# Second expert layer: chunks prepared rank by rank, table work later on VectorE, and 32 identity products ahead of the second half's counts

## Chip, cores and metric

One core of one Trainium2 chip. The metric is the time of one execution in device microseconds; for each kernel the median of the timed runs counts.

## What is computed

The input is x of 8 x 128 tokens with 256 features, and a context of the same shape. Four layers follow one another, each added to x: a long convolution over the features (by Toeplitz products), a mixture of 8 experts (2 per token), a cross attention with a latent width of 64, and a second mixture of 32 experts. The change is in that last layer:

```python
w, idx = _gate(xf, gate_w)            # sigmoid scores, 4 of 8 groups, then 6 of 32 experts
c = jnp.zeros((T, E), xf.dtype).at[jnp.arange(T)[:, None], idx].add(w)
g = jnp.einsum('td,eid->tei', xf, w11)
u = jnp.einsum('td,eid->tei', xf, w33)
act = jax.nn.silu(g) * u
y = jnp.einsum('tei,te,edi->td', act, c, w22)
shared = jax.nn.silu(xf @ sw1.T) * (xf @ sw3.T) @ sw2.T
return (y + shared).reshape(x.shape)
```

There T is 1024 tokens, E is 32, and an expert's hidden width is 128.

## The kernel before, in words

The kernel is written engine by engine, with every order and every semaphore by hand: one block each for SyncE (`sp`, which issues the loads), GpSimd (`pool`), ScalarE (`act`), VectorE (`dve`) and TensorE (`pe`).

**Routing.** Tokens are routed in two halves of four blocks. For each half TensorE makes the logits (`logits`, L1684), ScalarE the sigmoid, VectorE the choice of six experts a token (`choose`, ending in the mask at L1316), and TensorE counts how many rows stand ahead of each one (`count_rows`, L1712 and L1717). VectorE makes slots from the counts (`later_slots` for the second half, first instruction L1124). A token's six chosen experts, in the order of the expert's number, are its ranks 0 to 5. For each rank of a half, `stage_values` (L1161 to L1168) makes the slots and gate values, and GpSimd sends the four blocks' rows to DRAM by four indirect transfers (`send_rows`, L688). The sends of the second half are numbered 6 to 11, one per rank; before rank 3, 4 or 5 is staged, the rank three before it must have been sent, since they share a buffer.

**Chunks.** The rows of an expert lie in chunks of 224 (two tiles of 112). The first 32 chunks are the first of each expert, and their order is fixed. Chunk k holds only tokens of rank k or lower, so chunks 0 to 4 need the ranks up to their own number, and all chunks from 5 on need all six (`wait_sent`). Each chunk is one step s = 4i + r of a loop that all engines run (`run_steps`):

- SyncE loads the chunk's rows (`rowbuf`) and its weights (`up_raw`, `down_raw`; for experts 11 to 22 these were loaded early into buffers of their own).
- TensorE turns the rows (`turn_rows`, L1784); ScalarE copies the turned rows and the up weights to a short format (L843, L848, `high_parts`), and VectorE keeps the rests (L1416, L1421, `low_parts`). This is the preparation of a chunk.
- TensorE makes gate and up products (`up`, twelve products at L1664 to L1666); ScalarE applies silu (L870); VectorE copies the rows' targets (`place`, L1434) and multiplies (`hid`, L1443); TensorE makes the down product (`down`, L1817); ScalarE scales the results (`take_y`, L857), and GpSimd sends them back to the tokens' places in DRAM (L726), two transfers a chunk.

In the steady loop, TensorE's step s is: up of s, turn of s + 2, down of s - 1. The copy to `place` waits until the results of the chunk four before have been sent, since they read that buffer.

**What stands around the change.** Before the loop VectorE stages the second half's ranks (numbers 6 to 11), multiplies the shared expert's hidden values (`shared_hid`, L1373), adds the shared expert's output to x (`add_shared`, L1381), and works out which experts need a second chunk (`table_sums`, `table_turns` from L1202, `table_codes` from L1224 to L1239; the tables are read after 24 chunks). Only then come the preparations of chunks 0 and 1 (`low_parts`). TensorE makes the shared expert's products (`shared_up`, `shared_down` at L1749), waits until all of them have been added to x, because the second turned chunk shares a bank with them, and turns chunks 0 and 1 one after the other. In step r of the first four, it does up r, down r - 1, turn r + 2. The function `keep_busy` (L1742) multiplies the identity by itself into a bank that nobody reads; it is called twice before, with six products each.

Of the kernel before, what the change touches and what calls it, by code (L numbers as in the profile page):

```python
# [49 lines left out]
def build(nc, x_d, ctx_d, ctxr_d, filt_d, skip_d, wr_d, up0_d, down0_d, theta_d, theta_b_d, phi_d, phi_b_d, g_d, g_b_d,  # L50
# [11 lines left out]
    with ExitStack() as stack:  # L62
# [241 lines left out]

        def run_steps(eng, n, step):

            for i in range(FIXED[n]):
                for r in range(4):
                    step(i, r, i == 0, False)
            turns, more = load_turns(eng, n)  # L310
            with eng.Fori(FIXED[n], more + (MINT[n] - 1)) as i:
                for r in range(4):
                    step(i, r, False, False)
            for r in range(4):
                step(more + (MINT[n] - 1), r, False, True)
            return turns

        def prepared(n):

            def ahead_of(r, prepare):
                if n == 0 and r < 2:
                    for t in range(2 * r):
                        prepare(t)
                else:
                    prepare(r)

            return ahead_of

        def is_zero(count):
# [95 lines left out]
        def _(sp):  # L427
# [41 lines left out]
            for n in range(2):  # L469
# [70 lines left out]
                def step(i, r, first, last):  # L540
# [5 lines left out]
                    down_src = None if own else of_unit(down_d, here, r % upe)  # L546
                    if not (last and r >= 2):
                        c, first_unit, _, cslot, _ = chunk_of(n, i, r, 2)
                        slot, _ = step_slot(i, r, 2)
                        up_src, rows_src = None if own_later else of_unit(up_d, later, r % upe), rows_of(region)  # L550
                        if not first:

                            sp.wait_ge(f.w_split, s - 1)
                        elif r >= 2:
                            sp.wait_ge(f.w_split, r - 1)
                            if upe == 1:
                                sp.wait_ge(f.x_split, r - 1)
# [8 lines left out]
                    if not first and not own:  # L566
                        sp.wait_ge(f.down_done, s - 3)
                        load(down_raw[r][:], down_src, f.down_in[r])
# [183 lines left out]
        def _(act):  # L752
# [56 lines left out]
            for n in range(2):  # L809
# [52 lines left out]
                high_parts(0, 0, 0)  # L862
                high_parts(0, 1, 0)

                def step(i, r, first, last):
                    s = 4 * i + r
                    if n == 0 and first and r == 2:
                        take_y(i, r, -1)
                    act.wait_ge(f.up_done, s + 1)
                    nc.scalar.activation(silu_g[r % 2][:, 0:CHUNK[n]], gate_up(n, r % 2)[0][:, 0:CHUNK[n]], ACT.Silu)\  # L870
                        .then_inc(f.silu_made, 1)
                    if first:
                        if r and not (n == 0 and r == 2):
                            take_y(i, r, -1)
# [121 lines left out]
        def _(dve):  # L996
# [386 lines left out]
            for n in range(2):  # L1383
                f, upe = ffns[n], UPE[n]
                ahead_of = prepared(n)
                if n == 0:
                    for c in range(4):
                        split_rows(0, c)
                    route_first()
                else:  # L1390
                    stage_values(6)
                    shared_hid(1)
                    stage_values(7)
                    stage_values(8)
                    shared_hid(2)
                    table_sums(1, 2)
                    stage_values(9)
                    shared_hid(3)
                    add_shared(0)
                    table_turns(1, 2)  # L1400
                    stage_values(10)
                    add_shared(1)
                    stage_values(11)
                    table_codes(1)

# [17 lines left out]

                low_parts(0, 0, 0)
                low_parts(0, 1, 0)

                def step(i, r, first, last):
# [16 lines left out]
                    ins.then_inc(f.hid_made, 1)  # L1444
                    if first:
# [4 lines left out]
                turns = run_steps(dve, n, step)  # L1450
                last_k = TOPK[n] - 1
# [173 lines left out]
        def _(pe):  # L1625
# [128 lines left out]
            for n in range(2):  # L1754
# [14 lines left out]
                if n == 1:  # L1769
# [4 lines left out]
                    shared_down(3)  # L1774
                    pe.wait_ge(x_added, X_ATT1 + 4)

# [46 lines left out]
                turn_rows(0, 0, 0)  # L1823
                if upe == 1:
                    turn_rows(0, 1, 0)

                def turn_later(i, r):
                    c, first_unit, _, _, _ = chunk_of(n, i, r, 2)
# [3 lines left out]
                    turn_rows(i, r, 2)  # L1832

                def step(i, r, first, last):
                    if first:
                        if n == 0 and r == 2:
                            down(i, r, -1)
# [145 lines left out]
                shared_down(0)  # L1983
                logits(1)
                count_rows(1, slice(4, B), RANKS[1][1], 3)

# [54 lines left out]
```

## Time and profile before

| What | us |
|---|---|
| three timed runs | 410.45, 412.38, 405.9 |
| their median | 410.45 |
| the profiled execution's own time | 408.52 |
| its span, from first to last instruction | 406.7 |

The span is read from the first to the last instruction of one execution; the time of that execution is 1.8 us longer. Over the span the mean granted clock of TensorE was 0.849 of 2.4 GHz, where the levels are 2.4 and 1.2 GHz. TensorE is busy 71% of the span, VectorE 63%, GpSimd 52%, ScalarE 41%. The convolution layer ends near 68 us, the first expert layer near 179 us, the attention and the routing of the second layer near 300 us, and the rest is the loop over 32 chunks and the sum at the end.

### The profile page before, as it was taken

Reading aid. Unit: us, or ns where it says so; the run is one execution under the profiler, and the core shown is the slowest. Engines: PE = TensorE matmul, PEld = TensorE weight load, DVE = VectorE, ACT = ScalarE, POOL = GpSimd, SP = SyncE. Lnnn points to the kernel's source line nnn. Section 1 sums busy time; section 2 is a strip of 40 time slices with the busy share of each in tenths; the row PEclk is TensorE's granted clock in tenths of the full one; section 3 lists DMA queues with packets and bytes.
Section 4 is the critical chain, followed back from the end, with each engine's and each line's share of the span. In section 5 each row is a group of like instructions: output and inputs, shape, how many; then the busy total and the mean of one; then the engine's idle time right before and its main releaser. Section 6 shows DMA issues by size and latency. Waiting matters only on the chain.

```text
span 406.7 us, 5245 instructions
## 1 busy us (share of the span) xinstructions
PE 287.6 (71%) x1471; PEld 216.1 (53%) x1471; DVE 257.0 (63%) x758; ACT 167.7 (41%) x368; POOL 211.5 (52%) x238
## 2 busy tenths in 40 slices
PE   0899975610699999339899396583579899999600
PEld 0444433310679888026466174462569799998400
DVE  4499998570253533175886878798645566656366
ACT  1500003530255554525636534220266688887400
POOL 2577751037433555410511077767775677778830
PEclk9999997655599999958967778789598999999955
DMA  8556699723376651489989222325469855798598
GB/s 236 163 139 180 178 271 270 222 84 116 124 218 196 187 175 50 147 282 319 305 256 365 78 79 92 106 89 178 146 182 289 250 168 156 240 283 274 176 374 283
DMA packets 66062, 80.56 MB, mean 198 GB/s; under 512 B 7643, under 2 KB 55061, under 8 KB 66035
## 3 DMA queue, kind: packets, MB, share of 16 engines
q1 hardware_dynamic: 56547, 62.45, 52.2%
q0 software_dynamic: 7296, 16.93, 12.2%
q10 hardware_dynamic: 2192, 0.86, 0.8%
q8 instruction: 12, 0.20, 0.2%
q14 instruction: 15, 0.12, 0.1%
HBM read 43.70 MB, written 38.01 MB: 201 GB/s over the span
## 4 chain that ended last, share of the span: by engine, by line
PE 52%; DVE 15%; DMA 11%; POOL 10%; issue 7%; ACT 4%; POOLq 1%; SPq 0%; ACTq 0%; DVEq 0%
PE banks L1817 9%; POOL rows_s L688 7%; PE banks L1664 6%; PE banks L1665 5%; PE banks L1666 5%; DMA y_s<-y_sb,place 4%; PE banks L1784 4%; PE banks L1645 4%; PE banks L1646 3%; PE banks L1647 3%; PE banks L1674 2%; POOL y_s L726 2%; DMA rowbuf<-rows_s 2%; PE banks L1910 2%; DMA pre_own<-y_s 2%
## 5 line engine op out<-in xcount | busy, mean ns | idle before, releaser
L726 POOL DMA_INDIRECT y_s<-y_sb,place x88 | 90.8, 1032 | 47.1 <-ACT y_sb L857 24.1
L688 POOL DMA_INDIRECT rows_s<-staged,slot_i x64 | 64.2, 1003 | 57.2 <-DVE staged L1168 38.9
L1664 PE MATMUL banks<-xT_hi,w_hi 128*128 128x224 f32 (+1 forms) x192 | 63.8, 332 | 8.2 <-DVE w_lo L1421 8.0
L1665 PE MATMUL banks<-xT_lo,w_hi 128*128 128x224 f32 (+1 forms) x192 | 56.5, 294 | 0.0
L1666 PE MATMUL banks<-xT_hi,w_lo 128*128 128x224 f32 (+1 forms) x192 | 56.4, 294 | 0.0
L1664 PEld LDWEIGHTS banks<-xT_hi,w_hi 128*128 128x128 f32 x192 | 38.5, 201 | 13.9 <-DVE w_lo L1421 10.9
L1817 PE MATMUL banks<-down_raw,hid 128*104 128x256 f32 (+1 forms) x176 | 44.0, 381 | 1.6 <-DVE hid L1443 1.4
L1784 PE MATMUL banks<-ident,rowbuf 112*128 112x112 f32 (+1 forms) x176 | 25.3, 275 | 27.2 <-DMA rowbuf<-rows_s 22.7
L765 ACT ACTIVATE h_sb<-x_sb,shift,rstd 128x256 f32<-128x256 f32 x22 | 11.7, 590 | 68.8 <-DVE shift L1027 68.8
L857 ACT ACTIVATE y_sb<-banks,meta 112x256 f32<-112x256 f32 (+1 forms) x88 | 36.3, 471 | 8.0 <-PE banks L1817 7.5
L1665 PEld LDWEIGHTS banks<-xT_lo,w_hi 128*128 128x128 f32 x192 | 38.5, 201 | 0.7
L640 POOL TENSOR_TENSOR kv<-ctxr_sb 128x512 f32<-128x512 f32 x32 | 32.6, 1041 | 11.4 <-PE banks L1647 11.4
L1666 PEld LDWEIGHTS banks<-xT_hi,w_lo 128*128 128x128 f32 x192 | 38.4, 200 | 0.0
L843 ACT ACTIVATE xT_hi<-banks 128x448 fp32r<-128x448 f32 (+1 forms) x40 | 22.9, 573 | 36.1 <-PE banks L1784 34.7
L870 ACT ACTIVATE silu_g<-banks 128x224 f32<-128x224 f32 (+1 forms) x48 | 18.3, 381 | 44.6 <-PE banks L1666 44.6
L1784 PEld LDWEIGHTS banks<-ident,rowbuf 112*128 112x128 f32 (+1 forms) x176 | 19.9, 151 | 28.9 <-DMA rowbuf<-rows_s 20.1
L1817 PEld LDWEIGHTS banks<-down_raw,hid 128*104 128x104 f32 (+1 forms) x176 | 28.1, 173 | 7.2 <-DVE hid L1443 1.7
L1413 DVE COPY meta<-rowbuf 112x4 f32<-112x4 f32 (+1 forms) x40 | 7.3, 183 | 34.2 <-ACT xT_hi L843 21.8
L1434 DVE COPY place<-meta 112x2 int32<-112x2 int32 (+1 forms) x40 | 7.6, 191 | 33.7 <-DMA y_s<-y_sb,place 17.1
L619 POOL TENSOR_TENSOR rstd<-veps,minus_half 128x4 f32<-128x4 f32 x8 | 8.6, 1070 | 38.6 <-DVE veps L1021 38.6
L1416 DVE TENSOR_TENSOR xT_lo<-banks,xT_hi 128x448 fp32r<-128x448 f32 (+1 forms) x40 | 26.1, 654 | 0.0
L1421 DVE TENSOR_TENSOR w_lo<-up_raw,w_hi 128x512 fp32r<-128x512 f32 x36 | 24.4, 683 | 0.0
(241 smaller groups left out, 595.5 us busy)
## 6 DMA issues: line engine op xcount, KB each, us to landing
rows_s<-empty SPq DMA_DIRECT2D x5, 2730.0 KB
up_raw<-in_up SPq DMA_DIRECT2D x38, 256.0 KB, 4.7
rowbuf<-rows_s SPq DMA_DIRECT2D x32, 227.5 KB, 3.4
down_raw<-in_down SPq DMA_DIRECT2D x38, 128.0 KB, 4.6
rows_s<-empty SPq DMA_DIRECT2D x7, 633.8 KB
rowbuf<-rows_s SPq DMA_DIRECT2D x8, 316.9 KB
toep<-filt_s SPq DMA_DIRECT2D x16, 128.0 KB, 3.3
h_sb<-y_s SPq DMA_DIRECT2D x4, 512.0 KB, 5.3
```

Of the source, the lines that this page charges most:

```text
L640: last = nc.gpsimd.tensor_tensor(kv[slot][:, blk].rearrange("p (b i j) -> p b i j", i=HD, j=HD), k, v, ALU.mult)
L688: nc.gpsimd.indirect_dma_start(out=rows_s, out_offset=bass.IndirectOffsetOnAxis(ap=slot_i[:, k, b:b + 1], axis=0), in_=staged[:, b, k % BU ...
L726: nc.gpsimd.indirect_dma_start(out=y_s[n], out_offset=bass.IndirectOffsetOnAxis(ap=place[slot][0:TILE[n], t:t + 1], axis=0), in_=y_sb[slot ...
L843: nc.scalar.activation(xT_hi[par][:, 0:KB * CHUNK[n]].rearrange("p (k c) -> p k c", k=KB), turned(n, par), ACT.Copy)\
L857: last = nc.scalar.activation(y_sb[slot][0:TILE[n], t], y_home(n, slot % 2, t), ACT.Copy, scale=meta[slot][0:TILE[n], t, 0:1])
L1416: nc.vector.tensor_tensor(xT_lo[par][:, cols].rearrange("p (k c) -> p k c", k=KB), turned(n, par), xT_hi[par][:, cols].bitcast(f32).rearra ...
L1421: nc.vector.tensor_tensor(w_lo[slot % 2][:], up_home(n, c, slot), w_hi[slot % 2][:].bitcast(f32), ALU.subtract).then_inc(f.w_split, 1)
L1664: nc.tensor.matmul(out, wh, xh, start=start, stop=False)
L1665: nc.tensor.matmul(out, wh, xl, start=False, stop=False)
L1666: return nc.tensor.matmul(out, wl, xh, start=False, stop=stop)
L1784: last = nc.tensor.transpose(turned(n, slot % 2)[:, k, t * TILE[n]:(t + 1) * TILE[n]], rowbuf[slot][0:TILE[n], t, k * P:(k + 1) * P], iden ...
L1817: last = nc.tensor.matmul(y_home(n, cslot % 2, t), hid[slot % 2][:, t * TILE[n]:(t + 1) * TILE[n]], down_home(n, c, slot), start=first_uni ...
```

## The change

It has four parts.

1. TensorE gets 32 products of the identity (`keep_busy`) between the second half's logits and its counts. They write to the bank of the counts, which is overwritten by them.
2. The first six chunks are prepared rank by rank, on TensorE, ScalarE and VectorE (`by_rank`, `prepares`). Only chunk 0 is prepared ahead of the loop. Step 0 prepares chunk 1, step 1 chunk 2, step 2 chunk 3, step 3 chunk 4, step 4 chunks 5 and 6 with chunk 4's down product between them, and step 5 chunk 7. TensorE's wait for the shared expert's sum now stands behind chunk 0's up products.
3. On VectorE chunk 0's split stands ahead of stage number 10, and all of step 0 ahead of stage number 11. The two table pieces are moved into the loop, behind steps 8 and 10.
4. SyncE asks for chunk 5's up weights and chunk 4's down weights before it waits for rank 5, no longer after it.

```diff
+        def by_rank(n, i, r):
+            return n == 1 and isinstance(i, int) and 4 * i + r < TOPK1
+        def prepares(i, r):
+            return ((1,), (1,), (1,), (1,), (1, 2), (2,))[4 * i + r]
...
 # SyncE
-                    if not (last and r >= 2):
+                    if n == 1 and first and r == 3:
+                        sp.wait_ge(f.w_split, 2)
+                        load(up_raw[1][:], of_unit(up_d, TOPK1 - 1, 0), f.up_in[1])
+                        sp.wait_ge(f.down_done, 1)
+                        load(down_raw[0][:], of_unit(down_d, TOPK1 - 2, 0), f.down_in[0])
+                        sp.wait_ge(f.x_split, 2)
+                        wait_sent(TOPK1 - 1)
+                        load(rowbuf[1][0:TILE[n], 0:TILES[n]], rows_of(TOPK1 - 1), f.rows_in[1])
+                    elif not (last and r >= 2):
...
 # ScalarE
+                    if by_rank(n, i, r):
+                        if 0 < s < TOPK1 - 1:
+                            take_y(i, r, -1)
+                        high_parts(i, r, prepares(i, r)[0])
+                        if s == TOPK1 - 2:
+                            take_y(i, r, 0)
+                            high_parts(i, r, 2)
+                        return
...
 # VectorE
-                    add_shared(0)
-                    table_turns(1, 2)
-                    stage_values(10)
-                    add_shared(1)
-                    stage_values(11)
-                    table_codes(1)
...
+                    if by_rank(n, i, r):
+                        for ahead in prepares(i, r):
+                            low_parts(i, r, ahead)
...
+                    if n == 1 and isinstance(i, int) and s == 8:
+                        table_turns(1, 2)
+                    if n == 1 and isinstance(i, int) and s == 10:
+                        table_codes(1)
...
+                    add_shared(0)
+                    low_parts(0, 0, 0)
+                    stage_values(10)
+                    add_shared(1)
+                    step(0, 0, True, False)
+                    stage_values(11)
...
 # TensorE
-                    pe.wait_ge(x_added, X_ATT1 + 4)
...
-                if upe == 1:
-                    turn_rows(0, 1, 0)
...
+                    if by_rank(n, i, r):
+                        s = 4 * i + r
+                        up(i, r, first)
+                        if 0 < s < TOPK1 - 1:
+                            down(i, r, -1)
+                        if s == 0:
+                            pe.wait_ge(x_added, X_ATT1 + 4)
+                        turn_later(i, r, prepares(i, r)[0])
+                        if s == TOPK1 - 2:
+                            down(i, r, 0)
+                            turn_later(i, r, 2)
+                        return
...
                 logits(1)
+                keep_busy(RANKS[1][1], 32)
                 count_rows(1, slice(4, B), RANKS[1][1], 3)
```

TensorE before, from the shared expert's last down products (`down_raw,hid` 128x256) over the turns (`ident,rowbuf`) to chunk 0's up products:

```order
L1749 MATMUL banks<-down_raw,hid 128x256 x8
L1784 MATMUL banks<-ident,rowbuf 128x112 x8
L1664 MATMUL banks<-xT_hi,w_hi 128x224
L1665 MATMUL banks<-xT_lo,w_hi 128x224
L1666 MATMUL banks<-xT_hi,w_lo 128x224
```

The same place now:

```order
L1786 MATMUL banks<-down_raw,hid 128x256 x8
L1820 MATMUL banks<-ident,rowbuf 128x112 x4
L1701 MATMUL banks<-xT_hi,w_hi 128x224
L1702 MATMUL banks<-xT_lo,w_hi 128x224
L1703 MATMUL banks<-xT_hi,w_lo 128x224
```

Eight turns, of chunks 0 and 1, have become four, of chunk 0; chunk 1's stand behind chunk 0's twelve up products.

VectorE before, from the sum of the shared expert's first half (`x_sb,banks`) over the first table instructions (`expert_f` and others):

```order
L1381 TENSOR_TENSOR x_sb<-x_sb,banks 128x512 x2
L1202 TENSOR_TENSOR expert_f<-sums_T 1x38
L1203 TENSOR_SCALAR expert_f<-expert_f 1x38
L1204 TENSOR_SCALAR is_last<-expert_f 1x38
L1205 TENSOR_TENSOR expert_f<-expert_f,is_last 1x38
L1206 TENSOR_TENSOR total_f<-cend 1x1
```

The same place now, with chunk 0's split and the start of stage number 10:

```order
L1408 TENSOR_TENSOR x_sb<-x_sb,banks 128x512 x2
L1425 COPY meta<-rowbuf 112x4
L1428 TENSOR_TENSOR xT_lo<-banks,xT_hi 128x448
L1433 TENSOR_TENSOR w_lo<-up_raw,w_hi 128x512
L1393 COPY staged<-ids 128x4
L1188 SCALAR_TENSOR_TENSOR pick<-nth,slot_f 128x128
```

The table instructions have gone from here, and the split of chunk 0 (`xT_lo`, `w_lo`) has come from behind stage 11. Where the table instructions stand now, behind chunk 10's split in step 8 and ahead of chunk 9's `place` and `hid`:

```order
L1433 TENSOR_TENSOR w_lo<-up_raw,w_hi 128x512
L1229 TENSOR_TENSOR expert_f<-sums_T 1x38
L1230 TENSOR_SCALAR expert_f<-expert_f 1x38
L1231 TENSOR_SCALAR is_last<-expert_f 1x38
L1232 TENSOR_TENSOR expert_f<-expert_f,is_last 1x38
L1233 TENSOR_TENSOR total_f<-cend 1x1
L1237 SCALAR_TENSOR_TENSOR extra_f<-chunk_no 1x38
L1239 SCALAR_TENSOR_TENSOR expert_f<-expert_f,extra_f 1x38
L1242 TENSOR_SCALAR extra_f<-chunk_no 1x15
L1243 TENSOR_SCALAR extra_f<-extra_f,total_f 1x15
L1244 TENSOR_REDUCE more_f<-extra_f 1x1
L1246 TENSOR_SCALAR last_f<-more_f 1x1
```

Eleven instructions of the table stand within a step of the loop; nine more (`table_codes`) stand two steps later in the same way.

## Rows read from the trace of the kernel before

**Rows 1.** GpSimd's timeline: start us, us, engine, line, operation [idle before, releaser].
```profile
268.72 1.15 POOL L688 DMA_INDIRECT rows_s<-staged,slot_i  x1 [1.93 <-DVE staged L1168]
...
298.77 1.37 POOL L688 DMA_INDIRECT rows_s<-staged,slot_i  x1 [0.30 <-issue]
300.44 0.97 POOL L726 DMA_INDIRECT y_s<-y_sb,place  x1 [0.30 <-ACT y_sb L857]
...
326.17 0.94 POOL L726 DMA_INDIRECT y_s<-y_sb,place  x1 [0.72 <-ACT y_sb L857]
...
329.16 0.94 POOL L726 DMA_INDIRECT y_s<-y_sb,place  x1 [0.30 <-issue]
```

**Rows 2.** The chain of waits, in order of time: start us, us, what.
```profile
301.71 2.87 DMA rowbuf<-rows_s
...
312.44 7.32 DMA y_s<-y_sb,place
...
389.62 5.67 DMA y_s<-y_sb,place
```

**Rows 3.** TensorE's timeline, chunks 0, 4, 5, 6 and 9.
```profile
290.81 0.55 PE L1664 MATMUL banks<-xT_hi,w_hi 128*128 128x224 f32 x1 [4.72 <-DVE w_lo L1421]
...
304.72 0.98 PE L1784 MATMUL banks<-ident,rowbuf 112*128 112x112 f32 x4 [2.40 <-DMA rowbuf<-rows_s]
305.38 0.54 PE L1664 MATMUL banks<-xT_hi,w_hi 128*128 128x224 f32 x1
...
308.03 0.55 PE L1784 MATMUL banks<-ident,rowbuf 112*128 112x112 f32 x4
...
309.09 0.45 PE L1664 MATMUL banks<-xT_hi,w_hi 128*128 128x224 f32 x1
...
311.68 0.46 PE L1664 MATMUL banks<-xT_hi,w_hi 128*128 128x224 f32 x1
...
321.56 0.37 PE L1664 MATMUL banks<-xT_hi,w_hi 128*128 128x224 f32 x1
```

**Rows 4.** VectorE's timeline: first and last of both table pieces; chunks 6 and 7.
```profile
278.92 0.18 DVE L1202 TENSOR_TENSOR expert_f<-sums_T 1x38 f32<-1x38 f32 x1
...
281.03 0.14 DVE L1219 TENSOR_SCALAR last_f<-more_f 1x1 f32<-1x1 f32 x1
...
287.33 0.38 DVE L1224 TENSOR_SCALAR is_last<-chunk_no,last_f 1x38 f32<-1x38 f32 x1
...
289.41 0.14 DVE L1239 CAST more_i<-more_f 1x1 int32<-1x1 f32 x1
...
313.79 0.17 DVE L1434 COPY place<-meta 112x2 int32<-112x2 int32 x1 [0.72 <-ACT silu_g L870]
...
319.85 0.35 DVE L1434 COPY place<-meta 112x2 int32<-112x2 int32 x1 [4.20 <-DMA y_s<-y_sb,place]
```

**Rows 5.** Busy time by stretch; behind GpSimd's: granted clock, DMA share, GB/s.
```profile
255.00:260.00 5.00, 1.06 (x10) 0.95 (x9) 4.02 (x29) 2.68 (x4) 3.78 (x5) 1.00 0.28 101
...
300.00:305.00 5.00, 2.60 (x20) 2.13 (x19) 1.66 (x5) 2.39 (x6) 3.78 (x5) 0.96 0.58 176
305.00:310.00 5.00, 5.00 (x31) 4.85 (x30) 2.56 (x8) 2.81 (x7) 2.21 (x3) 0.70 1.03 290
```

**Rows 6.** TensorE's timeline: six identity products, what follows them, and the counts.
```profile
239.70 1.51 PE L1742 MATMUL banks<-ident 128*128 128x128 f32 x12
241.14 1.98 PE L1929 MATMUL banks<-tx,outw_sb 64*128 64x512 f32 x4
...
260.96 0.47 PE L1712 MATMUL banks<-mask_r,before_r 128*128 128x128 f32 x1 [4.89 <-DVE mask_r L1316]
```

**Rows 7.** VectorE's timeline: its first use of the counts.
```profile
263.17 0.19 DVE L1124 TENSOR_SCALAR cend<-banks 128x32 f32<-128x32 f32 x1 [0.62 <-PE banks L1717]
```

**Rows 8.** The page's costliest groups: line, engine, operation, count | busy us, mean ns | idle before.
```profile
L843 ACT ACTIVATE xT_hi<-banks 128x448 fp32r<-128x448 f32 (+1 forms) x40 | 22.9, 573 | 36.1 <-PE banks L1784 34.7
...
L1421 DVE TENSOR_TENSOR w_lo<-up_raw,w_hi 128x512 fp32r<-128x512 f32 x36 | 24.4, 683 | 0.0
```

More of the change, by code:

```diff
@@ L303, in chunk_of, with run_steps @@
             return 2 * i + t // 2, t % 2 == 0, t % 2 == 1, (t // 2) % 2, i + t // 4
-        def run_steps(eng, n, step):
+        def run_steps(eng, n, step, begun=0):
             for i in range(FIXED[n]):
-                for r in range(4):
+                for r in range(0 if i else begun, 4):
                     step(i, r, i == 0, False)
@@ L322, in ahead_of @@
             def ahead_of(r, prepare):
[L323 to L327, printed above, removed]
-            return ahead_of
+                for t in range(2 * r) if r < 2 else (r,):
+                    prepare(t)
+            return ahead_of
+        def by_rank(n, i, r):
+            return n == 1 and isinstance(i, int) and 4 * i + r < TOPK1
+        def prepares(i, r):
+            return ((1,), (1,), (1,), (1,), (1, 2), (2,))[4 * i + r]
         def is_zero(count):
@@ L565, in step @@
                             load(up_raw[slot][:], up_src, f.up_in[slot])
-                    if not first and not own:
+                    if not first and not own and not (n == 1 and isinstance(i, int) and s == TOPK1 - 2):
                         sp.wait_ge(f.down_done, s - 3)
@@ L862, in _ @@
                 high_parts(0, 0, 0)
-                high_parts(0, 1, 0)
+                if n == 0:
+                    high_parts(0, 1, 0)
                 def step(i, r, first, last):
@@ L871, in step @@
                         .then_inc(f.silu_made, 1)
+                    if by_rank(n, i, r):
[6 more added lines that the diff above has]
+                        return
                     if first:
-                        if r and not (n == 0 and r == 2):
+                        if r and r != 2:
                             take_y(i, r, -1)
@@ L1389, in _ @@
                     route_first()
[L1390 to L1398, printed above, removed]
-                    add_shared(0)
-                    table_turns(1, 2)
-                    stage_values(10)
-                    add_shared(1)
-                    stage_values(11)
-                    table_codes(1)
                 def low_parts(i, r, ahead):
@@ L1422, in low_parts @@
                                             ALU.subtract).then_inc(f.w_split, 1)
-                low_parts(0, 0, 0)
-                low_parts(0, 1, 0)
                 def step(i, r, first, last):
@@ L1444, in step @@
                     ins.then_inc(f.hid_made, 1)
-                    if first:
+                    if by_rank(n, i, r):
+                        for ahead in prepares(i, r):
+                            low_parts(i, r, ahead)
+                    elif first:
                         ahead_of(r, lambda t: low_parts(i, t, 2))
@@ L1448, in step @@
                         low_parts(i, r, 2)
-                turns = run_steps(dve, n, step)
+                    if n == 1 and isinstance(i, int) and s == 8:
+                        table_turns(1, 2)
+                    if n == 1 and isinstance(i, int) and s == 10:
+                        table_codes(1)
+                if n == 0:
+                    low_parts(0, 0, 0)
+                    low_parts(0, 1, 0)
+                else:
+                    stage_values(6)
+                    shared_hid(1)
+                    stage_values(7)
+                    stage_values(8)
+                    shared_hid(2)
+                    table_sums(1, 2)
+                    stage_values(9)
+                    shared_hid(3)
+                    add_shared(0)
+                    low_parts(0, 0, 0)
+                    stage_values(10)
+                    add_shared(1)
+                    step(0, 0, True, False)
+                    stage_values(11)
+                turns = run_steps(dve, n, step, n)
                 last_k = TOPK[n] - 1
@@ L1823, in _, with turn_later @@
                 turn_rows(0, 0, 0)
-                if upe == 1:
-                    turn_rows(0, 1, 0)
-                def turn_later(i, r):
-                    c, first_unit, _, _, _ = chunk_of(n, i, r, 2)
+                def turn_later(i, r, ahead=2):
+                    c, first_unit, _, _, _ = chunk_of(n, i, r, ahead)
                     back = (1, 2)[n]
@@ L1831, in turn_later @@
                         pe.wait_ge(f.x_split, c - back + 1)
-                    turn_rows(i, r, 2)
+                    turn_rows(i, r, ahead)
                 def step(i, r, first, last):
+                    if by_rank(n, i, r):
[10 more added lines that the diff above has]
+                        return
                     if first:
-                        if n == 0 and r == 2:
+                        if r == 2:
                             down(i, r, -1)
```

## The prediction

> **What bounds the kernel now.** I read the chain of waits first, then the timelines of GpSimd, TensorE and VectorE between 255 and 330 us, and last the windows. No engine is full over the span, so the question is which one each stretch waits for.
>
> From 268.72 to 300 us it is GpSimd. It sends the second half's rows to their slots, six ranks of four transfers, back to back: the first at 268.72 after a wait of 1.93 us for VectorE, the last at 298.77, the first result row at 300.44 [rows 1]. From first to last that is 23 steps in 30.05 us, 1.31 us each (1.27 where nothing disturbs), so a rank comes every 5.1 to 5.2 us. Chunk k of the expert loop needs ranks 0 to k. Chunk 5, the last that waits for a rank, starts its load at 301.71 and takes 2.87 us [rows 2]; TensorE waits 2.40 us for it and turns it at 304.72 [rows 3].
>
> Meanwhile TensorE loses time that costs nothing yet: it multiplies chunk 0 only at 290.81, after 4.72 us of waiting for VectorE's splits, which stand behind its table work [rows 3]. But when chunk 5's rows are there, chunk 4's up products (305.38 to 308.03, at the low clock) still stand ahead of chunk 5's, which start at 309.09 [rows 3]. That work could lie in the wait. From there a chunk takes 2.59 us (309.09 to 311.68) [rows 3].
>
> Behind it comes a second loss. Chunk 7's hidden product needs the place buffer that chunk 3's results leave; they are sent at 312.44, take 7.32 us [rows 2], and VectorE stands 4.20 us until 319.85 [rows 4]. TensorE should have begun chunk 9 at 309.09 + 4 x 2.59 = 319.45 and begins at 321.56 [rows 3]: 2.1 us lost. The transfers are slow because the DMA engines are full in this stretch (share 1.03 of their time) [rows 5].
>
> From chunk 9 on GpSimd works without waiting: it still waits 0.72 us for chunk 8's results (326.17), none from 329.16 on [rows 1], and the last result transfer leaves at 389.62 [rows 2]. So TensorE's delays of some tenths behind chunk 9 are hidden by GpSimd, while a head start at chunk 8 is passed on to the end.
>
> **The change, part by part.** *The 32 products.* They stand on TensorE between the second half's logits and its counts. The counts start at 260.96, after 4.89 us idle, so the logits end near 256.0 [rows 6]. A product of the identity is two records: six of them took 239.70 to 241.14 at full clock, 0.24 us each [rows 6]. 32 of them: 7.7 us, from 256.0 to 263.7. That is 2.7 us past the time at which the mask is there. The counts then run at full clock. Now VectorE gets them 2.21 us after their start (260.96 to 263.17) [rows 6, 7]; at twice the clock between 1.1 and 2.2 us, I take 1.2, near the half, because nine short products are nearly all of it. VectorE starts on them at 264.9 instead of 263.17: 1.7 us late (bounds 1.6 and 2.7). It had waited only 0.62 us for the counts [rows 7], so a quicker count alone could have given at most that. All that follows on VectorE up to the first send is one chain, so GpSimd's 24 sends shift by 1.7 us: chunk 5's rows are loaded at 306.3 instead of 304.6. The shared expert's products behind the counts run at full clock, but nothing waits for them in this stretch.
>
> The Trainium skill prices these products differently. "TensorE: Matmul & The Clock Gate", section "Back-to-back issue gap", gives some 81 ns for a sustained product with 128 columns; by it 32 take an estimated 2.6 us, end within the idle 4.89 us and cost nothing. Its figure belongs to two-byte operands; these are four-byte ones, and the row above decides.
>
> *Chunks rank by rank.* Up 0 no longer waits for the tables; each of the first chunks is turned when its rows land. One chunk's cycle, up, down before it, turn, copies and splits, from rows: up 1.53 us (2.59 less the 1.06 from 308.03 to 309.09, which are turn and down [rows 3]), down 0.7 of these; then ScalarE copies the results (some 0.9) and the turned rows (0.57), and VectorE splits the rows and the weights (0.68 for the weights [rows 8], the rows about as long), 2.8 us with the turn hidden beside them. That is 5.0 us, against a rank every 5.1: it just keeps pace at full clock, without a reserve. So up 4 is done when rank 5 lands, and up 5 starts some 2.7 us after 306.3 (a turn instead of the results' copy, the rest as above), at 309.0: where it stands now. The 1.7 us head start of the reordering is what the products eat. One thing is left: down 4 has been done before up 5, so up 6 follows a turn only, 0.7 us early.
>
> *Loads.* Chunk 5's up weights and chunk 4's down weights (256 and 128 KB) are asked for before the wait for rank 5, about 1.3 us of transfer at 290 GB/s [rows 5] that leaves the crowded stretch.
>
> *Result transfers.* They start 1.7 us later, at 302.1, and follow each other every 1.25 us (0.94 and 0.30 of issue [rows 1]). The results of chunk 3 are now ready in time, so its second transfer leaves at 302.1 + 7 x 1.25 = 310.9, 1.5 us before 312.44. Chunk 4's leaves at 313.4; with a transfer as slow as 7.32 us it lands at 320.7 and holds chunk 8. The stall shrinks by 0 to 2.1 us; near the row of 7.32 us I take 0.3 for it, so that up 10 is some 1.0 us early with the 0.7 from above.
>
> *VectorE's tables move into the loop.* 11 instructions from 278.92 to 281.17 and nine from 287.33 to 289.5 [rows 4], 2.25 and 2.2 us, now follow chunks 8 and 10. In the loop VectorE has 0.72 us of idle time a chunk, so its five instructions of step 6 run from 313.79 to 313.79 + 2.59 - 0.72 = 315.7 [rows 4]; the products that need the last of them, chunk 8's, may start at 311.68 + 2 x 2.59 = 316.9 [rows 3]: 1.2 us of slack. The first group runs 2.25 - 0.72 = 1.5 us over and costs TensorE 0.3; 0.8 of it is left at chunk 10, and the second makes that 0.8 - 0.72 + 2.2 = 2.3, which costs 1.1 us. Bounds: nothing, if a wait for a result transfer holds TensorE then anyway, and 3.0 us (both groups less their idle time). Of the 1.4 I take 1.1, since GpSimd's lag hides some.
>
> *Sum:* products 1.7 later, reordering 1.7 earlier, 0.7 and 0.3 earlier, tables 1.1 later: +0.1 us, no change. The profiled execution took 408.52 us (span 406.7), the median of the three timed runs is 410.45, 1.9 above. The forecast for the median is 410.4 us.
>
> **Rivals.** *The head start survives* (products cheap, as the page's price has it, or hidden). Then counts come up to 0.6 us early, up 5 starts at 306.8, 2.3 us early; with 0.7 and up to 2.1 of the stall, less 1.1 for the tables, 3 to 4 us: 406.9. For it: the idle 4.89 us and the wait of 2.40 us. Against it: the measured 0.24 us a product.
>
> *The clock falls in the rank stretch, slower.* With chunks 5.1 us apart TensorE rests about 2 us in each. In the present run it rested 2.40 us before 304.72, and the granted clock, 0.96 of full over 300 to 305 us, was down to 1.2 GHz for the next products: up 4 took 2.65 us instead of 1.53 [rows 3, 5]. At that level a cycle costs 2.65 + 1.4 + 3.0 = 7.0 us, 1.9 more than a rank. One slow chunk is half swallowed by what waits later; from two on it decides: up 5 some 4 us late, less the 1 to 2 us that the stall gives back, 3 us: 413.4. For it: cycle and rank are equal, so nothing is caught up. Against it: rests of about this size did not always bring it down, as before the counts: the clock was still full over 255 to 260 us, in which TensorE hardly worked [rows 5].
>
> *The products don't hold the clock.* The counts are then both late and slow, 1.0 us more, of which nothing returns: 411.4. Against it: six such products held 2.4 GHz.
>
> **How the numbers follow.** Forecast 0.52, head start 0.20, falling clock 0.22, no clock held 0.06. The forecast's own range is 1.5 us to either side; the rivals reach 3.5 below and 3.0 above. Three runs of the kernel spread from 405.9 to 412.4, so a median wanders by some 2 us: 405.5 to 414.5. A change of 2% is 8.2 us, about what a measurement of this kernel can tell from no change; no case reaches it. Only if several add to a wander is it passed: 0.03 faster, 0.93 within, 0.04 slower.
>
> **What would show it.** 64 records of the identity over some 7.7 us, the counts behind them at 2.4 GHz and VectorE waiting over 2 us for them; the first send 1.7 us later; chunk 0's up products some 7 us earlier; up 5 within 1 us of 309.1; a shorter stall before chunk 7's place copy; the tables behind chunks 8 and 10 with TensorE waiting for a split there. Wrong would be: sends not later, up 4 still unfinished when rank 5 lands, or a low clock in several of chunks 1 to 5.

## The result and the profile after

The changed kernel takes 414.25 us in the median of four runs (411.3 to 416.35), the kernel before 410.49 in as many (405.9 to 412.38): ratio 1.0124, 95% interval [1.0073, 1.0175]. A second measurement (i1 below) gave 1.0099 [1.0057, 1.0142]. It is slower by some 4 us, less than 2%, but the interval does not hold 1; the forecast was no change. The ratios leave out executions more than 1.5% above the fastest of their kernel; f1 below loses four of twelve that way (416.9 to 418.1 us), and over all its executions its ratio would be 1.010 instead of 1.007. The profiled execution took 415.03 us, its span is 413.2.

GpSimd's timeline of the changed kernel, first and last send of the second half's rows and its waits for results (columns as in [rows 1]):

```profile
272.08 1.15 POOL L706 DMA_INDIRECT rows_s<-staged,slot_i  x1 [4.12 <-DVE staged L1195]
...
301.84 0.96 POOL L706 DMA_INDIRECT rows_s<-staged,slot_i  x1 [0.30 <-issue]
...
310.27 0.94 POOL L744 DMA_INDIRECT y_s<-y_sb,place  x1 [2.11 <-ACT y_sb L875]
...
317.06 0.94 POOL L744 DMA_INDIRECT y_s<-y_sb,place  x1 [4.60 <-ACT y_sb L875]
...
324.43 0.94 POOL L744 DMA_INDIRECT y_s<-y_sb,place  x1 [2.65 <-ACT y_sb L875]
```

The sends are 3.36 us later than in [rows 1] and as dense (29.8 us from first to last). Behind them GpSimd now waits for results three times, 9.4 us in all. Before, it waited in the same stretch as follows, 5.8 us with the 0.72 of [rows 1]:

```profile
311.19 0.94 POOL L726 DMA_INDIRECT y_s<-y_sb,place  x1 [3.38 <-ACT y_sb L857]
...
323.14 1.05 POOL L726 DMA_INDIRECT y_s<-y_sb,place  x1 [1.70 <-ACT y_sb L857]
```

The cause is in TensorE's timeline of the changed kernel: the products, the counts, and the chunks that a rank brings.

```profile
258.15 7.39 PE L1779 MATMUL banks<-ident 128*128 128x128 f32 x64
265.30 0.31 PE L1749 MATMUL banks<-mask_r,before_r 128*128 128x128 f32 x1
...
285.56 0.37 PE L1701 MATMUL banks<-xT_hi,w_hi 128*128 128x224 f32 x1 [1.96 <-DVE w_lo L1433]
...
291.50 0.55 PE L1701 MATMUL banks<-xT_hi,w_hi 128*128 128x224 f32 x1 [1.96 <-DVE w_lo L1433]
...
294.20 1.91 PE L1853 MATMUL banks<-down_raw,hid 128*112 128x256 f32 x4
295.90 0.95 PE L1820 MATMUL banks<-ident,rowbuf 112*128 112x112 f32 x4
298.82 0.55 PE L1701 MATMUL banks<-xT_hi,w_hi 128*128 128x224 f32 x1 [1.96 <-DVE w_lo L1433]
...
306.14 0.37 PE L1701 MATMUL banks<-xT_hi,w_hi 128*128 128x224 f32 x1 [1.96 <-DVE w_lo L1433]
307.58 1.02 PE L1853 MATMUL banks<-down_raw,hid 128*112 128x256 f32 x4
308.44 0.55 PE L1820 MATMUL banks<-ident,rowbuf 112*128 112x112 f32 x4
311.29 0.49 PE L1701 MATMUL banks<-xT_hi,w_hi 128*128 128x224 f32 x1 [2.31 <-DVE w_lo L1433]
...
318.08 0.37 PE L1701 MATMUL banks<-xT_hi,w_hi 128*128 128x224 f32 x1 [1.05 <-DVE w_lo L1433]
```

The six rows of L1701 with a wait are the starts of chunks 0 to 5. No chunk waits for rows here: each waits 1 to 2.3 us for VectorE's split, the end of its own cycle. A cycle takes 5.15 us with fast products (306.14 to 311.29) and 7.32 with slow ones (291.50 to 298.82 and 298.82 to 306.14). In the slow one up is 2.70 us instead of 1.44, down 1.70 instead of 0.86, the turn 0.95 instead of 0.55. Chunk 5 starts at 318.08, against 309.09 in [rows 3]. The granted clock of the same stretch of the changed kernel (columns: window, its length, busy time and count of each engine, clock, DMA share, GB/s):

```profile
291.00:294.00 3.00, 2.50 (x12) 2.50 (x12) 2.02 (x8) 0.00 (x0) 2.34 (x3) 0.50 0.50 183
294.00:297.00 3.00, 2.86 (x10) 1.96 (x9) 0.46 (x2) 1.21 (x4) 2.14 (x3) 0.50 0.26 92
297.00:300.00 3.00, 1.18 (x5) 1.18 (x6) 1.29 (x3) 0.96 (x2) 2.39 (x3) 0.50 0.66 211
300.00:303.00 3.00, 3.00 (x13) 2.65 (x12) 0.46 (x2) 0.36 (x1) 2.19 (x3) 0.50 0.74 212
...
306.00:309.00 3.00, 2.85 (x20) 2.44 (x20) 0.54 (x3) 0.72 (x2) 1.85 (x2) 1.00 0.70 196
...
312.00:315.00 3.00, 3.00 (x13) 2.74 (x13) 0.44 (x2) 0.36 (x1) 0.46 (x1) 0.53 0.87 250
```

From 291 to 303 it is 0.50, 1.2 GHz. The same view of the kernel before:

```profile
291.00:294.00 3.00, 3.00 (x15) 3.00 (x16) 0.97 (x2) 0.26 (x1) 2.39 (x3) 0.50 0.60 189
294.00:297.00 3.00, 3.00 (x24) 2.81 (x23) 2.12 (x7) 1.82 (x5) 2.39 (x3) 0.95 0.35 94
297.00:300.00 3.00, 2.74 (x22) 2.27 (x21) 1.66 (x5) 2.49 (x7) 2.39 (x3) 1.00 0.81 248
```

That kernel starts its chunks late, when several ranks have landed, runs the first four with one rest of 0.26 us, and is back at 2.4 GHz behind the first chunk. The changed one starts 8.6 us earlier behind the first send (13.5 instead of 22.1) and rests in every cycle. VectorE's timeline of the changed kernel, with the mask, the first use of the counts, the places of chunks 5 to 7 and the first piece of table work in the loop:

```profile
262.93 0.23 DVE L1343 TENSOR_SCALAR mask_r<-marked 128x128 fp32r<-128x128 f32 x1
...
266.57 0.19 DVE L1151 TENSOR_SCALAR cend<-banks 128x32 f32<-128x32 f32 x1 [1.72 <-PE banks L1754]
...
320.11 0.41 DVE L1444 COPY place<-meta 112x2 int32<-112x2 int32 x1 [0.40 <-ACT silu_g L889]
321.90 0.17 DVE L1444 COPY place<-meta 112x2 int32<-112x2 int32 x1
324.44 0.19 DVE L1444 COPY place<-meta 112x2 int32<-112x2 int32 x1 [0.72 <-ACT silu_g L889]
...
328.80 0.18 DVE L1229 TENSOR_TENSOR expert_f<-sums_T 1x38 f32<-1x38 f32 x1
...
331.16 0.14 DVE L1246 TENSOR_SCALAR last_f<-more_f 1x1 f32<-1x1 f32 x1
331.33 0.17 DVE L1444 COPY place<-meta 112x2 int32<-112x2 int32 x1
```

The account between the two profiles, each in us later than before: the mask 2.25 (262.93 against 260.68; nothing that the diff touches lies ahead of it on VectorE, and in the profile of i1, the same kernel, it is at 261.18, so most of this is chance of the execution), the counts another 1.15 (3.64 behind the mask instead of 2.49), the rank stretch 5.6 (chunk 5 is 46.0 behind the first send instead of 40.4; in i1's profile 45.9). That makes 9.0 at chunk 5. Chunk 6 wins 0.8 back, as forecast, and the wait of 4.20 us ahead of chunk 7's place [rows 4] is gone (324.44 waits 0.72 for ScalarE), so chunk 9 is only 5.9 late, and the last result transfer leaves 6.6 late, 396.20 against 389.62 [rows 2]. Without the 2.25 us at the mask 4.35 us are the change's, near the 3.8 us between the two medians.

### The profile page after: what moved, and what is told of

The parts are those of the page before. It is cut to its first block, busy times and chain, and to the rows that moved or that the text cites. A ratio compares the mean times of both kernels' runs of the same rounds, so it can differ in the third digit from the quotient of the medians.

```text
span 413.2 us, 5371 instructions
## 1 busy us (share of the span) xinstructions
PE 299.1 (72%) x1535; PEld 226.2 (55%) x1535; DVE 256.8 (62%) x758; ACT 167.6 (41%) x368; POOL 211.5 (51%) x238
## 4 chain that ended last, share of the span: by engine, by line
PE 50%; DVE 16%; POOL 10%; DMA 10%; issue 7%; ACT 4%; POOLq 1%; SPq 0%; ACTq 0%; DVEq 0%
PE banks L1853 9%; POOL rows_s L706 7%; PE banks L1701 5%; PE banks L1702 5%; PE banks L1703 5%; DMA y_s<-y_sb,place 4%; PE banks L1682 4%; PE banks L1683 3%; PE banks L1684 3%; PE banks L1820 3%; PE banks L1779 2%; PE banks L1711 2%; POOL y_s L744 2%; PE banks L1957 2%; DVE stats L1039 2%
## 5 line engine op out<-in xcount | busy, mean ns | idle before, releaser
L1701 PE MATMUL banks<-xT_hi,w_hi 128*128 128x224 f32 (+1 forms) x192 | 64.1, 334 | 15.0 <-DVE w_lo L1433 14.9
L1701 PEld LDWEIGHTS banks<-xT_hi,w_hi 128*128 128x128 f32 x192 | 38.7, 201 | 22.0 <-DVE w_lo L1433 18.5
L1853 PE MATMUL banks<-down_raw,hid 128*104 128x256 f32 (+1 forms) x176 | 46.2, 395 | 0.3 <-DVE hid L1453 0.3
L1853 PEld LDWEIGHTS banks<-down_raw,hid 128*104 128x104 f32 (+1 forms) x176 | 29.3, 181 | 6.1 <-issue 0.7
```

The costliest lines, as they stand in the source:

```text
L1701: nc.tensor.matmul(out, wh, xh, start=start, stop=False)
L1853: last = nc.tensor.matmul(y_home(n, cslot % 2, t), hid[slot % 2][:, t * TILE[n]:(t + 1) * TILE[n]], down_home(n, c, slot), start=first_uni ...
```

## The experiments

Theory A: the clock falls in the rank stretch, since TensorE rests in each cycle. Theory B: the 32 products are the loss. The runs fell on two kinds of chip. On two chips (f on one, i on the other) the kernel before takes 410 us. On two others (e and g on one, h on the other) it takes 446, with long idle times that the profile puts down to no data and no other engine. Each ratio is to the kernel before on the same chip in the same batch. No kernel here leaves out any of the computation.

**Undo one part each (e1 to e4, a chip at 446 us).** e1 takes out the products:

```
-                keep_busy(RANKS[1][1], 32)
```

e2 adds that line alone to the kernel before. e3 adds to the changed kernel six products of the identity behind the turns of chunks 1 to 4; e4 moves the table work:

```
                         turn_later(i, r, prepares(i, r)[0])
+                        if s < TOPK1 - 2:
+                            keep_busy(7, 6)
...
-                    if n == 1 and isinstance(i, int) and s == 8:
+                    if n == 1 and isinstance(i, int) and s == 1:
...
-                    if n == 1 and isinstance(i, int) and s == 10:
+                    if n == 1 and isinstance(i, int) and s == 2:
```

> The changed kernel without the 32 products; the rank by rank order, the loads and the moved tables stay. Theory A (the clock falls in the rank stretch; the products cost only their 1.1 to 1.7 us): first second-half send 1 to 2 us after its place before, but one or more of the ups of chunks 1 to 4 still at 1.2 GHz with a cycle of 7.3 us, ratio to the kernel before 1.005 to 1.011. Theory B (the products are the whole loss): ratio 0.990 to 1.001.

> The kernel before with nothing but the 32 products ahead of the second half's counts. Theory A: counts reach VectorE 1.1 to 1.7 us later after the mask than before, all sends shift by that, ratio 1.002 to 1.006. Theory B: ratio 1.010 to 1.015, as the changed kernel.

> The changed kernel with six more products of the identity behind the turns of chunks 1 to 4, into a bank that nobody reads, so that TensorE works in the rest of 2 us ahead of the next up products. Theory A: chunks 1 to 4 stay at 2.4 GHz (at most one of them slow), up 5 is 3 to 6 us earlier than in the changed kernel as counted from the first second-half send, ratio to before 0.998 to 1.006. Theory B and the theory that the tables cost it: no better than the changed kernel, 1.010 or more.

> The changed kernel with the two table pieces behind steps 1 and 2, where VectorE waits over 2 us a chunk, instead of behind steps 8 and 10. Theory A: a gain of 0.5 to 1.5 us over the changed kernel at most, ratio to before 1.009 to 1.013. If the tables in the loop are the main cost: ratio 1.003 or less.

Measured: e1 1.0275 [1.0215, 1.0335], e2 1.0170 [1.0108, 1.0232], e3 1.0228 [1.0148, 1.0309], e4 1.0291 [1.0228, 1.0354]. Every one is slower than the kernel before, the products alone by 1.7%, and all but e3, which only lies above theory A's range, lie above the ranges of both theories; these were written for a chip at 410 us. Here is what the products meet, TensorE's timeline of e2:

```profile
258.70 3.98 PE L1742 MATMUL banks<-ident 128*128 128x128 f32 x32
263.13 0.37 PE L1742 MATMUL banks<-ident 128*128 128x128 f32 x1 [0.45 <-issue]
265.25 0.27 PE L1742 MATMUL banks<-ident 128*128 128x128 f32 x1 [1.75 <-issue]
267.38 0.27 PE L1742 MATMUL banks<-ident 128*128 128x128 f32 x1 [1.85 <-issue]
```

Half of the products run densely, then TensorE stands up to 1.85 us ahead of single ones. "issue" means that the profile shows nothing that it waits for; that it waits for its instructions is likely, but not shown. VectorE has the counts 5.96 us behind the mask there, 3.5 later than without products, where the whole kernel is 7.6 us slower; the rest is not explained. For the chips at 410 us that says nothing, so the same kernels ran there.

**The same on a chip at 410 us (f1 to f4).** f1 is e1, f2 is e2, f3 is e3; f4 is e3 without the 32 products and with e4's tables.

> The changed kernel without the 32 products, once more, since the four runs before were timed on a chip on which every kernel took 36 us longer. Theory A (the clock falls in the rank stretch): ratio 1.004 to 1.012, ups of two or more of chunks 1 to 4 at 1.2 GHz. Theory B (the products are the loss): ratio 0.990 to 1.001.

> The kernel before with nothing but the 32 products. Theory A: ratio 1.002 to 1.006, VectorE uses the counts 1.1 to 1.7 us later behind the mask. Theory B: 1.010 to 1.015.

> The changed kernel with six products of the identity behind the turns of chunks 1 to 4. Theory A: chunks 2 to 4 at 2.4 GHz with a cycle near 5.1 us instead of 7.3, ratio 0.998 to 1.006. Theory B: 1.010 or more.

> The rank by rank order without the 32 products, with six filler products behind the turns of chunks 1 to 4, and the table pieces behind steps 1 and 2. Theory A: this takes away the low clock, the late counts and the tables in the crowded part of the loop: ratio 0.988 to 0.998, up 5 at 36 to 39 us behind the first second-half send (40.4 before). Theory B: the same, since the products are gone; it differs from f1 by nothing.

Measured: f1 1.0073 [1.0024, 1.0121], f2 1.0022 [0.9984, 1.0061], f3 1.0002 [0.9969, 1.0036], f4 1.0003 [0.9960, 1.0046]. Theory B falls: the products alone make no difference that this measurement shows, and without them most of the loss stays. In f1 chunk 5 starts 45.6 us behind the first send, with slow cycles of 7.3 and 6.8 us at chunks 1, 3 and 4. With the six filler products it is 40.9 (f3), and the loss is gone. f4 missed its range of 0.988 to 0.998: without the products and with the tables early it is no better than f3, so the gain that theory A expected beyond the lost clock is not there.

**Filler without the 32, a filler in the kernel before, fewer products, tables early (g1 to g4, then h1 to h4 as repeats).** g1 has both edits of e1 and e3. g2 changes the kernel before; g3 is e3 with a shorter row of products; g4 is e4.

```
+                        if n == 1 and r == 3:
+                            keep_busy(7, 9)
                         ahead_of(r, lambda t: turn_later(i, t))
...
-                keep_busy(RANKS[1][1], 32)
+                keep_busy(RANKS[1][1], 18)
```

> The changed kernel without the 32 products and with six products of the identity behind each of the turns of chunks 1 to 4 (the tables stay behind chunks 8 and 10). Theory 'falling clock': with the clock held in the rank stretch the head start of the new order survives, and without the 32 products nothing eats it: ratio to the kernel before 0.993 to 1.000, chunk 5's up products 40 to 42 us behind the first send, cycles of chunks 1 to 5 of 5.1 to 5.3 us. Rival 'the filler itself is in the way': six products are 1.4 us in each of four cycles; if they delay the path, the ratio is above 1.003 and chunk 5 is over 43 us behind the first send.

> The kernel before with nine products of the identity (2.2 us at full clock) in the wait of 2.40 us ahead of chunk 5's turn, nothing else. Theory 'falling clock': the low clock behind that wait cost chunk 4's up products 1.1 us; held, chunk 5's up products start about 1 us earlier behind the first send (40.4 us in the profile of before, 39.3 here), and the first up products behind the wait take some 1.5 us a chunk instead of 2.65; ratio 0.996 to 1.000. Rival 'the clock follows something else': the products do not change the spacing of chunk 4's up products, ratio 1.000 to 1.003.

> The changed kernel with 18 products instead of 32 between logits and counts (4.3 us at full clock, within the idle 4.89 us) and the six in each rank step. If the lateness that the 32 cause is their length beyond the mask, VectorE uses the counts 1.8 to 2.2 us behind the mask (3.6 with 32, 2.5 with none), and the ratio is 0.993 to 0.999. Rival 'the clock is what delays the counts whatever stands ahead': 2.5 us or more behind the mask and a ratio of 1.000 or above.

> The changed kernel with VectorE's two groups of table work behind chunks 1 and 2 instead of 8 and 10, the 32 products and the order of ranks as they are. Theory 'falling clock': the tables late in the loop cost about 0.4 us; early they lie in a stretch where the slow chunks set the pace: ratio 1.009 to 1.015, as the changed kernel's 1.012. Rival 'tables in the loop are the loss': they gave 3 us or more of the 3.8; ratio 1.001 to 1.005.

> As g1, on a chip where programs wait little for instructions. Falling clock: 0.993 to 1.000, chunk 5 at 40 to 42 us behind the first send. Filler in the way: above 1.003, over 43 us.

> As g2, on such a chip. Falling clock: chunk 5 about 39.3 us behind the first send (40.4 in before), 0.996 to 1.000. Rival: chunk 4's up products stay slow, 1.000 to 1.003.

> As g3, on such a chip. The 32 late by their length: counts used 1.8 to 2.2 us behind the mask, 0.993 to 0.999. Rival: 2.5 us or more, 1.000 or above. In g3 it was 2.5 us.

> As g4, on such a chip. Falling clock: 1.009 to 1.015. Tables in the loop are the loss: 1.001 to 1.005.

Both batches fell on chips at 446 us. Measured: g1 1.0151 [1.0092, 1.0211] and h1 1.0123 [1.0082, 1.0165]; g2 1.0066 [1.0027, 1.0105] and h2 1.0068 [1.0029, 1.0106]; g3 1.0135 [1.0088, 1.0182] and h3 1.0138 [1.0092, 1.0184]; g4 1.0239 [1.0198, 1.0280] and h4 1.0224 [1.0172, 1.0276], above both ranges again. Against e1's 1.0275, from another batch, the fillers give 1.2 to 1.5 points here too; the same kernel in three batches (e4, g4, h4) differs by up to 0.7. g3's and h3's counts are used 2.49 us behind the mask, as with no products at all, and their ratios are those of g1 and h1 within the intervals: products that end before the mask cost nothing that shows. My 1.8 to 2.2 us was wrong: the clock had fallen again by the time the mask came at 270.85 in g3 (18 products do not reach it; the granted clock was 0.50 over 269 to 271 us), so no gain was left. g2 and h2 missed what theory A expected, 0.996 to 1.000: nine products in the kernel before cost 0.7% there. They could not show what they were made for, since the wait that they should fill is missing on these chips. TensorE's turn of chunk 5, first in e2, which has the order of before and no filler there, then behind the filler in h2:

```profile
328.46 0.55 PE L1784 MATMUL banks<-ident,rowbuf 112*128 112x112 f32 x4
```

```profile
321.84 2.17 PE L1742 MATMUL banks<-ident 128*128 128x128 f32 x18
323.85 0.55 PE L1784 MATMUL banks<-ident,rowbuf 112*128 112x112 f32 x4
```

e2's turn has no idle time ahead of it, where [rows 3] has 2.40 us, and chunk 4 behind it takes 1.41 us (328.78 to 330.19), as fast as in h2: there was neither a wait to fill nor a low clock to lift, and the filler's 2.17 us stood in the way. Whether filling that wait pays at 410 us was not tried.

That g1 and h1 are slower than before, though h1's granted clock was 1.00 from 316 us on, seems to have its own cause. By their numbers, chunk 5 at 55.6 and 54.5 us behind the first send, they meet the rival "filler in the way"; i2 below, with 0.9990 and 41.4 us, does not. ScalarE's and GpSimd's timelines of h1:

```profile
307.92 0.36 ACT L889 ACTIVATE silu_g<-banks 128x224 f32<-128x224 f32 x1 [14.26 <-remote]
...
312.09 0.96 POOL L706 DMA_INDIRECT rows_s<-staged,slot_i  x1 [7.41 <-DVE staged L1195]
```

In h1 ScalarE stands 14.26 us ahead of chunk 0's silu, 11.2 of them after chunk 0's up products have ended at 296.76. In the new order VectorE's step 0 stands ahead of its last staging, `stage_values(11)`, so this wait is passed to the sends, which take 36.5 us instead of 29.5 (first to last, h1 against h2). In the order before, all staging is ahead of the expert loop, and the sends run through a wait just as long (h2: 14.57). The 7 us are 1.6% of this kernel and would account for the loss, but no run took them away. At 410 us nothing of this shows: 29.8 us from first to last send in the changed kernel.

**As changed, and fillers alone, on the chip at 410 us (i1, i2).** i1 is the changed kernel, i2 is g1.

> The changed kernel as it is, beside i2. On a chip with long waits for instructions (before at 446 us): its tables stand behind chunks 8 and 10, in h4 and g4 behind 1 and 2; falling clock: 1.020 to 1.028, as those (1.022 and 1.024); rival, tables in the loop are the loss: 1.032 or above. On a chip as the first (before at 410 us): 1.008 to 1.016.

> As h1. Before at 446 us: 1.010 to 1.017 again. Before at 410 us: 0.993 to 1.000, chunk 5 at 40 to 42 us behind the first send; filler in the way: above 1.003, over 43 us.

Measured: i1 1.0099 [1.0057, 1.0142], i2 0.9990 [0.9951, 1.0029]. The cycles of chunks 2 to 5 in i2, from TensorE's timeline:

```profile
295.30 0.38 PE L1701 MATMUL banks<-xT_hi,w_hi 128*128 128x224 f32 x1 [0.95 <-DVE w_lo L1433]
296.74 1.03 PE L1853 MATMUL banks<-down_raw,hid 128*112 128x256 f32 x4
297.60 0.55 PE L1820 MATMUL banks<-ident,rowbuf 112*128 112x112 f32 x4
297.99 1.52 PE L1779 MATMUL banks<-ident 128*128 128x128 f32 x12
300.46 0.37 PE L1701 MATMUL banks<-xT_hi,w_hi 128*128 128x224 f32 x1 [0.95 <-DVE w_lo L1433]
...
305.61 0.37 PE L1701 MATMUL banks<-xT_hi,w_hi 128*128 128x224 f32 x1 [0.95 <-DVE w_lo L1433]
...
310.77 0.37 PE L1701 MATMUL banks<-xT_hi,w_hi 128*128 128x224 f32 x1 [1.06 <-DVE w_lo L1433]
```

5.16, 5.15 and 5.16 us a chunk. The filler (1.52 us) lies in the rest of 1.96 and leaves 0.95 of it, so it delays nothing. And its clock over the same time, beside f1, which has neither products nor filler; first i2:

```profile
288.00:292.00 4.00, 4.00 (x21) 3.94 (x21) 2.35 (x9) 0.22 (x1) 3.08 (x4) 0.58 0.47 169
292.00:296.00 4.00, 3.05 (x25) 2.73 (x24) 1.75 (x5) 1.93 (x5) 3.09 (x4) 1.00 0.60 176
...
304.00:308.00 4.00, 3.05 (x23) 2.66 (x23) 1.65 (x5) 1.11 (x3) 2.83 (x3) 1.00 0.86 243
```

then f1:

```profile
288.00:292.00 4.00, 2.15 (x10) 2.15 (x11) 2.87 (x10) 0.99 (x2) 3.08 (x4) 0.50 0.54 170
292.00:296.00 4.00, 3.21 (x12) 2.31 (x11) 0.64 (x4) 1.86 (x5) 3.09 (x4) 0.53 0.51 158
...
304.00:308.00 4.00, 2.83 (x13) 2.21 (x12) 0.67 (x4) 1.88 (x5) 1.86 (x2) 0.75 0.65 180
```

The ratios to the kernel before, set side by side by what differs:

| the kernel before, products | no filler | six fillers a rank |
|---|---|---|
| 410 us, 32 products | 1.0124, 1.0099 (i1) | 1.0002 (f3) |
| 410 us, none | 1.0073 (f1) | 0.9990 (i2) |
| 446 us, 32 products | 1.0291, 1.0239, 1.0224 (e4, g4, h4, tables early) | 1.0228 (e3) |
| 446 us, none | 1.0275 (e1) | 1.0151, 1.0123 (g1, h1) |

Read across a row at 410 us, holding the clock is worth 0.8 to 1.2 points; read down a column, the products cost 0.1 to 0.5, which the intervals do not separate from nothing. At 446 us, where the cells come from several batches, only the fillers without the 32 products stand out, by 1.2 to 1.5. No version was shown to beat the kernel before: i2's interval holds 1.

## Why the prediction was wrong, point by point

The step that failed is the cycle: "it just keeps pace at full clock, without a reserve". The cycle was right, 5.0 us forecast and 5.15 measured, and so was the missing reserve. The words "at full clock" were not. Three of the cycles between chunks 1 and 5 ran mostly at 1.2 GHz (7.32, 7.32, 6.79 us; in i1's profile 7.29, 6.59, 6.39 and 6.01), nothing could be caught up, and chunk 5 came 46.0 us behind the first send where the forecast puts it at 38.6 (309.0 less 270.4). With the clock held it is 41.4 (i2). The rest to 38.6 is in the first two cycles: chunk 0 starts 13.5 us behind the first send, and five cycles of 5.15 make 39.2, but the filler did not hold the clock in the first ones, which took 6.2 us each.

The rival "the clock falls in the rank stretch, slower" is what happened. Its slow cycle of 7.0 us measured 7.32, its "some 4 us late" for chunk 5 was 5.6 (three slow cycles, not two), its 1 to 2 us given back by the stall were 2.2 (of the 3.1 us between chunks 5 and 9, 0.8 are chunk 6's), its time 413.4 stands against 414.25. The 0.22 it got was too low. I held against it that the clock was full over 255 to 260 us, where TensorE hardly worked [rows 5]. That window ends too early: over 261 to 263 us, behind the same idle time, the granted clock was 0.50, and the counts took 2.21 us there against 1.27 at 2.4 GHz. One row taken behind dense work is no evidence for a stretch of bursts and rests that goes on for 30 us; the nearest evidence was the row that I used for the rival, 2.40 us of rest and then slow products [rows 3].

The 32 products: forecast 1.7 us late, measured 1.15 (f2: 3.59 us behind the mask, i1: 3.62). Two records a product is right, 64 of them. They took 7.15 us from 258.15 to the counts, 0.223 each instead of 0.24, and that is the difference. The counts behind them took 1.27 us, as forecast (1.2). The 81 ns of the Trainium skill ("TensorE: Matmul & The Clock Gate", section "Back-to-back issue gap") would have given an estimated 2.6; the trace decides against it for these four-byte operands.

The head start of the order: forecast 1.7 us earlier. Even at a held clock and with no products to eat it none is left at chunk 5 (i2: 41.4 us behind the first send, against 40.4 before), and i2's ratio holds 1.

Chunk 6 behind a turn only: forecast 0.7 us early, measured 1.76 us behind chunk 5 instead of 2.59, 0.8. Right. Result transfers: forecast that the stall shrinks by 0 to 2.1, taken 0.3. It vanished, since chunk 7 itself came 8 us late, when VectorE had no transfer left to wait for; with chunk 6's 0.8 that is why 9.0 us at chunk 5 became 5.9 at chunk 9. The sum behind the 0.3 failed too: chunk 3's second transfer, forecast at 310.9, left at 318.31, because the slow cycles brought its results late. The step treated the stall as the transfers' matter only, and it belongs to whichever of the two comes last.

Tables in the loop: forecast 1.1 us. Their 2.5 us piece ends at 331.30, right ahead of a place copy, and TensorE's next chunk is 2.97 us behind its last instead of 2.59: 0.4 us; the second piece shows no longer step. Moved early they made no difference at 410 us (f4 beside i2: 1.0003 and 0.9990, with overlapping intervals). The rival in i1's expectation for the chip at 446 us stays untried, because i1 ran at 410.

That "up 0 some 7 us earlier" was right (8.6 behind the first send), and is part of the trouble: earlier work was also sparser work. The list of signs named the right one, "a low clock in several of chunks 1 to 5".

That 414.25 lies within the stated 405.5 to 414.5 is owed to the room given to a median's wander, not to the mechanism. The sum of +0.1 on 410.45 makes 410.55, not 410.4, which changes nothing.

## What to carry to other kernels

When a change lets TensorE start each piece of work as its data lands, compare the sum of a cycle's parts with the interval of arrival at both clock levels: if the full-clock cycle only just fits, the rests it opens can bring the clock down and the stretch then runs at its own slow pace. Work that starts late and in one dense run may end as early as work that starts early and rests. Filler products that fit into the rests gave the lost 0.8 to 1.2% back here, and no more than that. A filler pays only where the rest exists: put into the kernel before on chips where TensorE did not wait at that point, nine products cost 0.7%.

## What the runs showed that I had not expected

The same program of this kernel takes 410 us on two chips and 446 on two others. Part of the difference shows as idle time that no data and no other engine explains: over 11 of the 14.26 us ahead of one ScalarE instruction and up to 1.85 us ahead of single TensorE products in a row of 64. The 32 added products cost 1.7% there against 0.2%. What these chips do differently is not shown.

With a rest of about 2 us in each cycle of 7 the granted clock stayed at 0.50 through four rows of the view, 291 to 303 us, although TensorE was busy for 1.2 to 3.0 of their 3 us. With six fillers in the rest, which left 0.95 us idle in 5.15, it was 1.00 from 292 us on (i2). In the first two cycles, of 6.2 us each, it was still at 0.56 to 0.58 in the rows from 284 to 292 us with the fillers in place; why is not shown.

Between executions the mask, ahead of everything that the edits touch, came at 260.38 us in f3 and at 264.95 in f2. Two profiles can thus differ by over 4 us before the changed part begins, and positions are best read behind a common event, here the mask or the first send.
